# A graph kernel that counts its edges in 55 steps of 12 destinations in place of 40 steps of 16

## What is computed

```python
e = jnp.exp(-leaky_relu(al[src] + ar[dst], negative_slope=0.1))
h_prime = segment_sum(e[:, None] * h[dst], src, N) / (segment_sum(e, src, N)[:, None] + EPS)
x = layernorm(x + elu(h_prime))
for r in range(8):
    mask = (edge_type == r)
    sums = segment_sum(x[src] * mask[:, None], dst, N)
    cnt = segment_sum(mask, dst, N)
    out = out + (sums / maximum(cnt, 1)[:, None]) @ weight[r]
z = concatenate([u, x], 1) @ w_gate + b_gate
x = layernorm(tanh(u) * z + x * (1 - z))
```

## Time and profile before

| | us |
|---|---|
| median of 3 runs | 995.83 |
| lowest and highest | 995.46, 996.17 |
| profiled execution | 996.23 |
| its span, first to last instruction | 994.2 |
| PE busy | 980.8 |
| DVE busy | 391.7 |
| ACT busy | 281.3 |
| POOL busy | 254.3 |

### The profile page before, as it was taken

One profiled execution on the slowest core, in us unless ns is written; L12 is line 12 of the kernel. 1 busy time (PEld: TensorE's weight loads), 2 busy tenths in 40 slices (PEclk: granted clock), 3 DMA queues, 4 the chain that ended last, 5 costly groups with the idle time before them and its releaser, 6 DMA issues.

```text
span 994.2 us, 14628 instructions
## 1 busy us (share of the span) xinstructions
PE 980.8 (99%) x5159; PEld 825.1 (83%) x5159; DVE 391.7 (39%) x746; ACT 281.3 (28%) x487; POOL 254.3 (26%) x196
## 2 busy tenths in 40 slices
PE   9999999999999999999999999999999999999997
PEld 7866778788888888888888988988988988888886
DVE  7998773720332330430530440242232233202277
ACT  4325543741122122221221221222222212212432
POOL 0000002065323223223223132142232232326730
PEclk9999999999999999999999999999999999999999
DMA  7304657066211411411311321231141051212402
GB/s 265 95 13 119 177 143 239 1 225 199 79 40 33 154 41 42 141 51 42 131 62 42 108 84 42 74 118 33 27 165 33 20 170 34 73 52 66 138 1 103
DMA packets 69005, 91.41 MB, mean 92 GB/s; under 512 B 9396, under 2 KB 35475, under 8 KB 68838
## 3 DMA queue, kind: packets, MB, share of 16 engines
q1 hardware_dynamic: 68966, 90.90, 29.1%
HBM read 75.19 MB, written 15.69 MB: 91 GB/s over the span
## 4 chain that ended last, share of the span: by engine, by line
PE 94%; DVE 2%; ACT 1%; issue 1%; DVEq 0%; POOL 0%; ACTq 0%
PE ps L1188 21%; PE ps L1190 21%; PE ps L1189 21%; PE ps L1444 9%; PE ps L1443 9%; PE ps L1294 5%; PE ps L1256 1%; PE ps L1499 1%; PE ps L1498 1%; PE ps L1497 1%; PE ps L1269 1%; PE ps L1277 1%; PE ps L1271 1%; PE ps L1270 1%; PE ps L1432 0%
## 5 line engine op out<-in xcount | busy, mean ns | idle before, releaser
L469 POOL TENSOR_TENSOR w_lo<-w_raw,w_hi 128x512 fp32r<-128x512 f32 x168 | 217.4, 1299 | 697.9 <-ACT w_hi L544 546.6
L544 ACT CAST w_hi<-w_raw 128x512 fp32r<-128x512 f32 x184 | 114.7, 623 | 464.9 <-PE ps L1190 397.2
L1188 PE MATMUL ps<-w_hi,M_hi 128*128 128x512 f32 (+1 forms) x550 | 215.9, 393 | 0.1
L1190 PE MATMUL ps<-w_lo,M_hi 128*128 128x512 f32 (+1 forms) x550 | 214.6, 390 | 0.0
L1189 PE MATMUL ps<-w_hi,M_lo 128*128 128x512 f32 (+1 forms) x550 | 214.5, 390 | 0.0
L1062 DVE SCALAR_TENSOR_TENSOR u<-ps,scale,u 128x512 f32<-128x512 f32 (+1 forms) x90 | 66.4, 744 | 314.8 <-PE ps L1190 314.8
L1443 PE MATMUL ps<-C_hi,x_hi 128*128 128x320 f32 (+3 forms) x640 | 184.5, 306 | 0.0
L1444 PE MATMUL ps<-C_hi,x_lo 128*128 128x320 f32 (+3 forms) x640 | 184.4, 307 | 0.0
L1188 PE MATMUL ps<-w_hi,M 128*128 128x512 f32 (+1 forms) x360 | 140.4, 390 | 0.0
L1190 PE MATMUL ps<-w_lo,M 128*128 128x512 f32 (+1 forms) x360 | 140.4, 390 | 0.0
L1189 PE MATMUL ps<-w_hi,M 128*128 128x512 f32 (+1 forms) x360 | 140.4, 390 | 0.0
(11 more groups left out here) (178 smaller groups left out, 773.6 us busy)
## 6 DMA issues: line engine op xcount, KB each, us to landing
w_raw<-weights SPq DMA_DIRECT2D x184, 256.0 KB, 2.8
C_dram<-Cst SPq DMA_DIRECT2D x25, 512.0 KB, 6.3
C_hi<-C_dram SPq DMA_DIRECT2D x8, 1600.0 KB, 7.0
z<-b_gate SPq DMA_DIRECT2D x5, 512.0 KB, 9.6
u<-bias SPq DMA_DIRECT2D x5, 512.0 KB, 7.5
xT_raw<-xT SPq DMA_DIRECT2D x8, 312.5 KB, 6.5
u<-x SPq DMA_DIRECT2D x4, 512.0 KB, 4.9
last_raw<-weights SPq DMA_DIRECT2D x8, 256.0 KB, 5.6
```

What stands on the lines that cost most here:

```text
L469: pool.tensor_tensor(w_lo[k % RING][:, :], w_raw[k % RING][:, :], w_hi[k % RING][:, :].bitcast(f32), ALU.subtract).then_inc(w_lo_done, 1)
L544: nc.scalar.copy(w_hi[k % RING][:, :], w_raw[k % RING][:, :]).then_inc(w_hi_done, 1)
L1188: mm(o, lhs_hi[:, k, c], w_hi[k % RING][:, :], start=opens, stop=False)
L1190: last = mm(o, lhs_hi[:, k, c], w_lo[k % RING][:, :], start=False, stop=closes_)
```

## The change

A step has 12 destinations, so that its 40 codes fit one bank: HOT = 480 columns, one matmul. A tile of 128 destinations takes PER = 11 steps (the last one of 8), and there are 55. A pass has 4 tiles. Steps alternate between the banks 5 and 6. `win_edge`, a column with each step's first destination, takes 8 more small operations on DVE, each waiting for the one before. The integer of step w + 1 is read before the loop of step w, on both engines. The schedule's numbers become (before in brackets): E_W = 12, 14, 19, 30, 41 (12, 14, 18, 24, 32), MULT_W = 17, 28, 39, 50, 61 (16, 22, 30, 38, 46); the sums come at steps 11, 22, 33, 44 (8, 16, 24, 32). The items in steps 0 to 7, the draining and AL_W = 10 keep their step numbers.

```diff
-    BODY = 5
+    BODY = 4
...
-    WIN = P // R
-    WINDOWS = NP // WIN
-    PER = P // WIN
     CODES = NT * R
+    WIN = 512 // CODES
+    PER = -(-P // WIN)
+    WINDOWS = NT * PER
+    HOT = CODES * WIN
...
+    def win_at(w):
+        return P * (w // PER) + WIN * (w % PER)
+
+    def win_width(w):
+        return min(WIN, P - WIN * (w % PER))
...
-            MULT_W.append(max(E_W[j] + 4, PER * j + 14))
+            MULT_W.append(max(E_W[j] + 4, PER * (j + 1) + 6))
...
         def window_bank(w):
-            return 2 if w >= TWINS and (WINDOWS - w) % 2 == 0 else 5
-
-        def last_in_pair(w):
-            return max([v for v in range(w) if window_bank(v) == window_bank(w)], default=-1)
+            return 5 + w % 2
...
-            v.tensor_scalar(table[:, :], iota_i[:, :], 1.0 / (P // 2), None, ALU.mult)
+            v.tensor_scalar(table[:, 0:HOT], iota_i[:, 0:HOT], 1.0 / (P // 2), None, ALU.mult)
...
-            step(v.tensor_scalar(win_edge[:, 1:2], part_col[:, :], float(WIN), float(WIN - 1), ALU.mult, ALU.add))
+            step(v.tensor_scalar(win_edge[:, 1:2], part_col[:, :], float(PER), float(P - PER * WIN), ALU.is_ge, ALU.mult))
+            for j in range(1, NT):
+                step(v.tensor_tensor(win_edge[:, 0:1], win_edge[:, 0:1], win_edge[:, 1:2], ALU.add))
+                if j < NT - 1:
+                    step(v.tensor_scalar(win_edge[:, 1:2], part_col[:, :], float(PER * (j + 1)), float(P - PER * WIN), ALU.is_ge, ALU.mult))
+            step(v.tensor_scalar(win_edge[:, 1:2], win_edge[:, 0:1], float(WIN - 1), None, ALU.add))
...
-                    v.tensor_scalar(hot[:, s * NP:(s + 1) * NP], table[:, :], float(WIN * w),
+                    v.tensor_scalar(hot[:, s * HOT:(s + 1) * HOT], table[:, 0:HOT], float(win_at(w)),
...
+            next_pass = window_range(DVE_ENGINE, 0)
             for w in range(WINDOWS):
-                first_pass = window_range(DVE_ENGINE, w)
+                first_pass = next_pass
                 dve.reg_mod(tile_at, first_pass, STARTS)
+                if w < WINDOWS - 1:
+                    next_pass = window_range(DVE_ENGINE, w + 1)
...
                     pe.wait_ge(built[s], n)
-                    for c in range(2):
-                        last = mm(bank(window_bank(w) + c, c=SPLIT), oh_s[:, ds(edge + s * P, P)],
-                                  hot[:, s * NP + c * SPLIT:s * NP + (c + 1) * SPLIT],
-                                  start=False, stop=False, skip_group_check=True)
-                    last.then_inc(counted[s], 1)
+                    mm(bank(window_bank(w), c=HOT), oh_s[:, ds(edge + s * P, P)], hot[:, s * HOT:(s + 1) * HOT],
+                       start=False, stop=False, skip_group_check=True).then_inc(counted[s], 1)
...
+            next_pass = window_range(PE_ENGINE, 0)
             for w in range(WINDOWS):
-                first_pass = window_range(PE_ENGINE, w)
+                first_pass = next_pass
                 pe.reg_mod(edge_at, first_pass, STARTS)
                 pe.reg_mul(edge_at, edge_at, P)
-                pe.wait_ge(window_copied, last_in_pair(w) + 2)
...
+                if w < WINDOWS - 1:
+                    next_pass = window_range(PE_ENGINE, w + 1)
+                pe.wait_ge(window_copied, max(w, 1))
```

More of the change, by code:

```diff
@@ L134, in gat_rgcn_kernel @@
             att16 = sb("att16", [P, RING_A, NP], i16, early)
-            hot = sb("hot", [P, BODY * NP], bf16, early)
+            hot = sb("hot", [P, 5 * NP], bf16, early)
             all_r = sb("all_r", [P, PART_S * P], f32r, early)
@@ L318, in gat_rgcn_kernel @@
             E_W.append(max(AL_W + 2 + 2 * j, MULT_W[j - 2] + 2 if j >= 2 else 0))
-            MULT_W.append(max(E_W[j] + 4, PER * j + 14))
+            MULT_W.append(max(E_W[j] + 4, PER * (j + 1) + 6))
         def hp_w(j):
             return MULT_W[j] + 3 if j < NT - 2 else WINDOWS
-        TWINS = AL_W + 2
         def window_bank(w):
-            return 2 if w >= TWINS and (WINDOWS - w) % 2 == 0 else 5
-        def last_in_pair(w):
-            return max([v for v in range(w) if window_bank(v) == window_bank(w)], default=-1)
+            return 5 + w % 2
         PE_ENGINE, DVE_ENGINE = mybir.EngineType.PE, mybir.EngineType.DVE
@@ L454, in _ @@
         def _(pool):
-            pool.iota(iota_i[:, :], pattern=[[1, CODES], [P // 2, WIN]], base=0, channel_multiplier=0).then_inc(pool_consts, 1)
+            pool.iota(iota_i[:, 0:HOT], pattern=[[1, CODES], [P // 2, WIN]], base=0, channel_multiplier=0).then_inc(pool_consts, 1)
             pool.iota(part_col[:, :], pattern=[[0, 1]], base=0, channel_multiplier=1,
@@ L574, in copy_window @@
                 j, v = divmod(w, PER)
+                n = win_width(w)
                 act.wait_ge(window_counted, w + 1)
@@ L578, in copy_window @@
                     act.wait_ge(turned, 2 * (j - 1))
[L579 to L583, removed]
+                nc.scalar.copy(Cst[j % 2][:, :, :, v * WIN:v * WIN + n].rearrange("p m r d -> p (m r) d"),
+                               bank(window_bank(w), c=HOT).rearrange("p (q d) -> p q d", d=WIN)[:, :, 0:n]).then_inc(window_copied, 1)
             def copy_summed(j, part):
@@ L1292, in counts @@
                     pe.wait_ge(built[s], n)
-                    for c in range(2):
-                        last = mm(bank(window_bank(w) + c, c=SPLIT), oh_s[:, ds(edge + s * P, P)],
-                                  hot[:, s * NP + c * SPLIT:s * NP + (c + 1) * SPLIT],
-                                  start=False, stop=False, skip_group_check=True)
-                    last.then_inc(counted[s], 1)
+                    mm(bank(window_bank(w), c=HOT), oh_s[:, ds(edge + s * P, P)], hot[:, s * HOT:(s + 1) * HOT],
+                       start=False, stop=False, skip_group_check=True).then_inc(counted[s], 1)
                 pe.reg_add(turn, turn, 1)
                 pe.reg_add(edge_at, edge_at, BODY * P)
+            next_pass = window_range(PE_ENGINE, 0)
             for w in range(WINDOWS):
-                first_pass = window_range(PE_ENGINE, w)
+                first_pass = next_pass
                 pe.reg_mod(edge_at, first_pass, STARTS)
                 pe.reg_mul(edge_at, edge_at, P)
-                pe.wait_ge(window_copied, last_in_pair(w) + 2)
[L1306 to L1309, removed]
+                if w < WINDOWS - 1:
+                    next_pass = window_range(PE_ENGINE, w + 1)
+                pe.wait_ge(window_copied, max(w, 1))
+                mm(bank(window_bank(w), c=2), zeros[:, :], zeros[:, 0:2], start=True, stop=False, skip_group_check=True)
                 with pe.Fori(first_pass, LOOP_END, STARTS + BODY):
                     counts(w)
-                mm(bank(window_bank(w) + 1, c=2), zeros[:, :], zeros[:, 0:2], start=False, stop=True, skip_group_check=True)\
+                mm(bank(window_bank(w), c=2), zeros[:, :], zeros[:, 0:2], start=False, stop=True, skip_group_check=True)\
                     .then_inc(window_counted, 1)
```

## The result

| us | before | after |
|---|---|---|
| median of 4 runs | 995.64 | 1010.26 |
| lowest and highest | 995.10, 996.17 | 1009.14, 1011.36 |
| profiled execution | 996.23 | 1011.36 |
| its span | 994.2 | 1009.6 |
| counting stage: start, end, length | 51.62, 153.56, 101.94 | 52.09, 168.84, 116.75 |

A forecast was written before the change was run, and what follows sets the result against it. PE's queue was taken to bound steps with only counting, its array the busy ones. Steps from 8 on +17.4, steps 0 to 7 -5.2, less 0.7: +11.5 on 996.23, 1007.7 profiled, 1007.3 median; range 997 to 1011.5.

The forecast's parts named there:

- What bounds a bare step: In a step where PE has no work besides counting, PE's queue, not its array, sets the length.
- The reading holds the queue: Each step's integer reading stops the engine's queue for its whole 0.302 us, so reading ahead is worth 0.
- Rivals (1) and (2): The reading doesn't hold the queue: (1) +0.5, 996.3 us, chance 0.11; (2) also hots at 0.22, -5, 991 us, chance 0.07.
- The price of a bare step: A step where PE only counts falls from 1.74 to 1.48 us, bounds 1.40 to 1.56.
- the 0.13 for five matmuls less: PE's queue in a step with only counting: five matmuls less save 0.13 us, bounds 0.05 to 0.15.
- Steps 0 to 7: Array-bound steps at the start of the counting stage: each 0.58 us shorter, once more for a second pass, -5.2 us.
- Steps 8 to 10: Steps without other PE work but with draining on DVE: 1.0, 2.3 and 2.3, together 5.6 us.
- Steps 11 to 21: First block from the first sum on, with a second pass and the diagonal with its matmuls: 24.4 us.
- The other blocks: Steps 22 to 32 at 21.3 us, 33 to 43 at 22.6 with a second pass, 44 to 54 at 21.0.
- 0.7 taken off: Deduction from the stage's growth for flush readings hidden by the queue's lead behind busy steps: 0.7 us.
- Rival (3): PE's queue runs further ahead: steps with only counting average 1.3 us, +5, 1001 us; inside the forecast's chance of 0.80.
- Parts at nothing: Eight added `win_edge` operations, 1.5 us hidden by DVE's 1.91 us wait for ACT; ACT's narrower copies also cost nothing.

The follow-up runs named there:

- experiment 4: The changed kernel with counting matmuls of 240 columns, hots still built at 480, half of the counts left out: 1015.44 us, ratio 1.0194.
- experiment 3: Constants in the program in place of all readings on both engines: changed kernel 1001.15 us, ratio 1.0053; kernel before 993.97 us, ratio 0.9981.
- experiments 1 and 2: Changed kernel with each reading back at its own step: 1009.49 us; kernel before with each reading one step ahead: 995.67 us.
- experiment 7: The kernel before with all 40 readings at once on each engine, ahead of the counting loop: 1007.09 us, ratio 1.0108.
- experiment 5: The changed kernel with filler matmuls of 512 columns for PE in steps 8 to 10, into an unused bank: 1008.53 us, ratio 1.0124.

## Why the prediction was right, and where its sum was off

The forecast was 1007.3 us, in a range of 997 to 1011.5; the kernel takes 1010.26. Direction, mechanism and the choice among the rivals held, and the sum was 3.0 us short. Some of its parts are right only because two errors cancelled, and the time comes out near the upper end of the range. Point by point:

- **What bounds a bare step.** Held. Halving the array's work left it at 1.55 us (experiment 4), and taking the reading out took most of them to 1.37 to 1.5 us, the two moves of the constant included (experiment 3).
- **The reading holds the queue.** Held, and shown three ways: the matmul behind it starts when it ends, reading ahead is worth 0 on 55 and on 40 steps (experiments 1 and 2), and forty of them hold PE 11.09 us (experiment 7). Rivals (1) and (2), at 996.3 and 991, fall with it. The Trainium skill's rule that the next instruction is decoded only when a sequencer-only one has executed (Perfetto Trace Analysis, the section on sequencer-only instructions) agrees with the 141.8 behind the 141.4 + 0.299. Another statement of the Trainium skill, that engine instructions can be read and queued while a control instruction executes (Advanced Engine Details and Errata, Sequencer Loop), isn't seen for this instruction, as the matmul with zeros starts at 141.8 too.
- **The price of a bare step, 1.48 us.** Too low; it is 1.545. One tile less was right (0.13; the pace is 0.124). The term that was mis-sized is the 0.13 for five matmuls less: it is 1.74 - 0.124 - 1.545 = 0.07, with the one matmul with zeros in it. The sum took 0.026 for each matmul, though its own bound was 0.02, and no row priced one. 1.545 lies inside the bounds 1.40 to 1.56; the terms themselves give 1.46 as the lower one.
- **A hot every 0.254 us on DVE.** Held: four take 1.11 us, the last of them 0.34, so 0.257.
- **Steps 0 to 7, -5.2.** 24.45 went to 19.62, -4.8. Step 3 is 62.36 - 59.80 = 2.56, step 4 and later ones 2.33 to 2.35, as forecast.
- **Steps 8 to 10, 5.6.** 5.87.
- **Steps 11 to 21, 24.4.** 26.2, the largest error. Step 11 alone took 6.45 us; with the clock kept up it takes 3.97 (experiment 5). The prediction took the granted clock as given, since before it was 1.00 everywhere, and didn't ask what a PE that waits in steps 8 to 10 does to it.
- **The other blocks, 21.3, 22.6 and 21.0.** 21.8, 22.4 and 20.9. The forecast had the flush's delay in two steps of a block, the fourth and fifth at 2.2 us each, and the second one, with a transposition, at 1.3, "with the queue still ahead". It fell otherwise: in steps 22 to 26 the second takes 1.95 us, since the reading holds the start of the step behind it there too, the fourth 2.40 and the fifth 1.61. The five together are 10.7 us where the forecast had 10.5, and that is luck.
- **0.7 taken off** for the queue's lead behind busy steps. Not found: the last three blocks are 65.0 us together, and their forecast without it was 64.9. Rival (3), a queue that runs further ahead, falls too: it had bare steps at 1.3 us.
- **Parts at nothing.** `win_edge` held: DVE's wait fell by 1.5 us and its product started no later. The stage did start 0.47 us later, because the integers of the list landed later (DVE's L838 at 14.93 instead of 13.94 us). In the other profiled runs of 55 steps it starts at 51.0 to 51.8, so this isn't the change's.

Of the 3.6 us between the profiled execution (1011.36) and its forecast (1007.7), about 1.8 are steps 11 to 21, 0.7 the deduction, 0.5 the start, and the remaining 0.6 mostly the first eleven steps. The 0.065 us too little for each bare step was made up in the blocks by steps priced a little too high, which is luck as well.

## What to carry to other kernels

Count what an engine's queue does in a step of a hardware loop (register instructions, branches, readings) and set it against the array's work in that step: a step made narrower gains only while the array is the longer of the two, and every added step pays the queue in full. A reading of a value into a register belongs where the engine has work queued and no DMAs out of SBUF are under way (in the kernel before, that is worth 1.95 us at most); moving it ahead of the step, among instructions of the same queue, changes nothing. If a change leaves PE standing still in small pieces, look at its granted clock in the steps behind.

## What was not expected of the hardware

- **PE's clock fell inside a dense kernel, where PE had waited in small pieces.** After the change, steps 8 to 10 leave PE busy 1.81 of 3.00 us (75 to 78 us), and the clock is at the 1.2 GHz level (0.50) from 78 to 81, in both profiles of it; the bare steps from 113 to 122 us, with PE busy 6.49 of 9.00 us, kept 1.00. At the low level eight matmuls of the sums over the types take 2.91 us, and 1.65 us at full clock with the filler. With matmuls of half the width the mean over the whole stage was 0.74, and a kernel that did less work took 5 us more.
- **The releaser's name doesn't tell a reading.** The same delay was called "issue", "ACT Cst" and, once PE had no reading, "DVE hot".
- **A reading of 0.30 us becomes 0.9 to 1.1 us** while the DMAs write from SBUF at some 280 GB/s, on PE and on DVE. Where the flush is cut to 8 partitions it is back at 0.30, but for single ones of 0.97 to 1.24 us. These stand where the cut flush itself is written, from 102 to 105 and from 122 to 125 us, at only 46 and 54 GB/s. So it isn't the rate alone; what in the writing slows a reading stays open. Beside loads into SBUF at 121 GB/s (41 to 42 us, experiment 7) two readings of DVE took 0.32 and 0.31 us.
